# Attention and a state-space layer on one core: row maxima twelve steps ahead, other places for five groups of TensorE work, and the layer norm's Newton rounds moved from GpSimd to VectorE

## The reference, cut to what matters

```
# layer 0, per image, n = 4096 tokens, 32 query/key channels, 256 value channels
q, k, v = wq x + bq, wk x + bk, wv x + bv
attn    = softmax(q k, axis=-1)            # 4096 x 4096 per image
x1      = gamma * (v attn^T) + x
# layer 1, tokens of 256 channels
u  = (x1 - mean) * rsqrt(var + 1e-5) * norm_g + norm_b        # the layer norm
z, xBC, dt = split(in_w u);  xBC = silu(conv4(xBC) + conv_b)   # 4 groups of 128 channels
state = state * exp(dt*A) + (dt*x) B;  y = state C + Dp*x      # scan over the tokens
y = rmsnorm(y * silu(z)) * rms_w;  o = out_w y
out = x1 + o * sigmoid(se2(relu(se1(mean(o)))))
```

## Time and profile before

| what | value |
|---|---|
| median of three runs (lowest, highest) | 3107.33 us (3104.92, 3109.52) |
| time of the profiled execution | 3107.73 us |
| its span, first to last instruction | 3105.6 us |
| mean granted clock of TensorE | 0.979 of full speed |
| PE busy | 2928.8 us, 94% of the span |
| DVE busy | 2068.1 us, 67% |
| POOL busy | 1994.4 us, 64% |
| ACT busy | 1926.2 us, 62% |

### The profile page before, as it was taken

The page is one execution under the profiler, slowest core; times in us unless marked ns, Lnnn a source line. Parts: engine busy times, 40 slices in busy tenths (PEclk is TensorE's granted clock), DMA queues, the critical chain, the costliest instruction groups (busy, mean ns, idle before and its releaser), DMA issues. The chain is left out here.

```text
span 3105.6 us, 62448 instructions
## 1 busy us (share of the span) xinstructions
PE 2928.8 (94%) x20696; PEld 2256.1 (73%) x20696; DVE 2068.1 (67%) x3577; ACT 1926.2 (62%) x3806; POOL 1994.4 (64%) x3087
## 2 busy tenths in 40 slices
PE   6889999999999999999999999999999999999974
PEld 3767777777767777777777777777777777777752
DVE  5556666766766676666776667676766667776653
ACT  2556666666656666666665666666666666666642
POOL 2446665677665676666676666676777667777753
PEclk9999999999999999999999999999999999999985
DMA  3111111111311112122221122112121111112021
GB/s 121 53 32 43 47 58 58 32 49 55 98 71 65 58 65 89 68 78 75 91 84 37 65 72 87 65 68 89 40 90 36 50 64 45 68 50 70 35 96 68
DMA packets 102512, 200.94 MB, mean 65 GB/s; under 512 B 18768, under 2 KB 41936, under 8 KB 97808
## 3 DMA queue, kind: packets, MB, share of 16 engines
q1 hardware_dynamic: 98192, 195.08, 18.5%
q10 hardware_dynamic: 4000, 1.86, 0.2%
HBM read 131.21 MB, written 64.75 MB: 63 GB/s over the span
## 5 line engine op out<-in xcount | busy, mean ns | idle before, releaser
L727 POOL TENSOR_TENSOR p_lo<-p,p_hi 128x512 f16<-128x512 f32 x1024 | 1220.0, 1199 | 737.0 <-ACT p_hi L890 587.7
L883 ACT ACTIVATE p<-p_et 128x512 f32<-128x512 f32 x1024 | 614.6, 600 | 574.6 <-PE p_et L1141 511.1
L1159 PE MATMUL acc<-v_hi,p_hi 128*128 128x257 f16 x4096 | 954.5, 273 | 6.6 <-DVE work L1463 5.6
L1161 PE MATMUL acc<-v_lo,p_hi 128*128 128x256 f16 x4096 | 952.4, 273 | 0.0
L1419 DVE TENSOR_REDUCE maxes<-p_mx 128x1 f32<-128x1024 f32 x508 | 619.3, 1219 | 267.9 <-PE p_mx L1120 267.6
L890 ACT ACTIVATE p_hi<-p 128x512 f16<-128x512 f32 x1024 | 646.2, 631 | 8.3
L1167 PE MATMUL acc<-v_hi,p_lo 128*128 128x257 f16 x4096 | 622.8, 274 | 17.1 <-POOL p_lo L727 17.1
L1159 PEld LDWEIGHTS acc<-v_hi,p_hi 128*128 128x128 f16 x4096 | 403.6, 99 | 133.2 <-issue 71.8
L1161 PEld LDWEIGHTS acc<-v_lo,p_hi 128*128 128x128 f16 x4096 | 400.6, 98 | 103.3 <-issue 43.4
L1167 PEld LDWEIGHTS acc<-v_hi,p_lo 128*128 128x128 f16 x4096 | 399.9, 98 | 70.4 <-POOL p_lo L727 18.3
L1141 PE MATMUL p_et<-qs,kst 98*128 98x256 f16 x2048 | 393.1, 273 | 3.6 <-ACT p L883 2.9
(11 more groups left out here) (214 smaller groups left out, 4139.9 us busy)
## 6 DMA issues: line engine op xcount, KB each, us to landing
work<-rows_d SPq DMA_DIRECT2D x32, 1024.0 KB, 4.9
xin<-in_x_dram SPq DMA_DIRECT2D x48, 512.0 KB, 5.0
xr<-in_x_dram SPq DMA_DIRECT2D x32, 512.0 KB, 3.7
x_d<-x1c SPq DMA_DIRECT2D x31, 512.0 KB, 3.1
og_d<-og SPq DMA_DIRECT2D x29, 512.0 KB, 2.7
mix_x<-x_d SPq DMA_DIRECT2D x25, 512.0 KB, 4.7
mix_o<-og_d SPq DMA_DIRECT2D x24, 512.0 KB, 5.6
out_dram<-mix_o SPq DMA_DIRECT2D x24, 512.0 KB, 3.0
```

The source lines that it names most:

```text
L727: e.tensor_tensor(p_lo[:, n % RING, :], p32[:, n % P32S, :], p_hi[:, n % RING, :], ALU.subtract).then_inc(lo_pool, 1)
L883: e.activation(p32[:, n % P32S, :], p_et[:, :], ACT.Exp).then_inc(exp_done, 1)
L1159: e.matmul(acc[:, t, 0:C + 1], p_hi[:, r, at:at + P], v_hi[:, 2 * k + kk, 0:C + 1], start=(k == 0 and kk == 0), stop=False)
L1161: e.matmul(acc[:, t, 0:C], p_hi[:, r, at:at + P], v_lo[:, 2 * k + kk, :], start=False, stop=False, skip_group_check=True)
```

## The change

Four constants move fills: the third convolution group goes from step 20 to step 21, the first residual transpose from step 13 to step 5, the residual's bias from step 4 to step 2, and `AHEAD` goes from 10 to 12. With it the last pair of a half falls in step 2, the parts in step 4, and the first pair of the next half but one in step 4. As `K_MR` and `K_QR` get a new offset, the rows are filled in steps 7 and 23 and copied in steps 8 and 24. In slot 0 one more pair is computed early. The order of the fills in steps 3 to 9 becomes: x1T, x1T; y0, st0; xT; cb1; mr; y1, st1; uT, uT. By the rule of the two banks the xT now waits until y0 has been read (or, where there is one, the qk), and cb1 waits until st0 has.

The three Newton rounds of the layer norm are taken from POOL (14 operations) and written on DVE in step 3 (10 operations, a drain ahead of each). The semaphore from the guess to POOL goes away.

```diff
-K_XBC = (11, 16, 20, 26)
+K_XBC = (11, 16, 21, 26)
-K_XT = (13, 19)
-K_XB = 4
+K_XT = (5, 19)
+K_XB = 2
-AHEAD = 10
+AHEAD = 12
-K_PARTS, K_MR, K_QR = STEPS - AHEAD, STEPS - AHEAD + 2, STEPS - AHEAD + 3
+K_PARTS, K_MR, K_QR = STEPS - AHEAD, STEPS - AHEAD + 3, STEPS - AHEAD + 4
@@ pairs_at
-    early = {8: 0, 10: 1, 12: 2, 13: 3, 14: 4}
+    early = {8: 0, 9: 1, 10: 2, 12: 3, 13: 4, 14: 5}
@@ gpsimd
-            def norm(g):
-                e.wait_ge(ln_guess, g + 1)
-                e.tensor_scalar(nw[:, 2, :], mv[:, :, 0], -1.0, None, ALU.mult)
-                newton(nw)
-                e.tensor_tensor(nw[:, 4, :], nw[:, 2, :], nw[:, 3, :], ALU.mult).then_inc(ln_ready, 1)
@@ gpsimd step
-                if 0 <= s - 1 < G and K == K_LN + 2:
-                    norm(s - 1)
@@ vector stage_a
-                    rsqrt_guess(nw, nwi, mv[:, :, 1], 1.0, 1e-5).then_inc(ln_guess, 1)
+                    rsqrt_guess(nw, nwi, mv[:, :, 1], 1.0, 1e-5)
+                if K == K_LN + 2:
+                    for _ in range(3):
+                        e.drain()
+                        v.tensor_tensor(nw[:, 1, :], nw[:, 3, :], nw[:, 3, :], ALU.mult)
+                        e.drain()
+                        v.scalar_tensor_tensor(nw[:, 1, :], nw[:, 1, :], -0.5, nw[:, 0, :], ALU.mult, ALU.mult)
+                        e.drain()
+                        v.scalar_tensor_tensor(nw[:, 3, :], nw[:, 1, :], 1.5, nw[:, 3, :], ALU.add, ALU.mult)
+                    e.drain()
+                    v.scalar_tensor_tensor(nw[:, 4, :], mv[:, :, 0], -1.0, nw[:, 3, :], ALU.mult, ALU.mult)\
+                        .then_inc(ln_ready, 1)
```

More of the change, by code:

```diff
@@ L394, in conv_attention_mamba_kernel @@
         filled = sem("filled")
-        ln_guess = sem("ln_guess")
         ln_ready = sem("ln_ready")
```

## The result

| | before | changed |
|---|---|---|
| median of five runs (lowest, highest) | 3107.33 us (3104.92, 3109.52) | 3198.24 us (3188.55, 3201.65) |
| ratio with its 95% interval | 1 | 1.0289 [1.0274, 1.0305] |
| span of the profiled execution | 3105.6 us | 3195.2 us |
| mean granted clock | 0.979 | 0.969 |

The forecast was 3128 us, in 3082 to 3148. The sign and the first cause were right, the size was not: the loss is 4.4 times the one forecast.

A forecast was written before the change was run, and what follows sets the result against it. PE, busy 94% of the span, was taken as the bound, so only its idle time could be won. Terms -26.1 - 1.9 - 12.7 + 4 - 4.5 + 64.8 - 3 = +20.6 us on 3107.7 gave 3128 us, range 3082 to 3148.

The forecast's parts named there:

- the first cause: PE's new wait in step 5, for DVE to read y0, eats up more than is won; chance 0.57.
- What bounds the kernel, and what goes: PE busy 94% of the span; five waits inside the slots, 47.0 us together, could be won.
- the second rival: The cover holds: the ten Newton operations hide in DVE's 2.79 us gap and the slack behind it; 3063.5 us, chance 0.10.
- the third: The gain isn't there: group 2's product late by 1.1 us in step 26 instead of 0.2; 3148 us, chance 0.10.
- The wait for the parts: The rows' fill waits for the parts of the maximum; to go in all slots, -26.1 us, bounds 0 to -26.1.
- the state's reader in step 13: First residual transpose (xT) leaves the crowded step 13 and its wait there ends, -4.5 us.
- the one behind the rows' copy in step 9: Layer norm transpose's 3.7 us wait: rows copied in step 8 stand before the mixing operations, half saved, -1.9 us.
- Newton on DVE: Collisions with POOL make the chain 6.2 us; PE waits in step 5, 2.4 us in 24 slots, 1.8 in four: +64.8.
- Third group at 21: Product's wait in step 20 goes, -12.7 us; group 2's product 0.2 us late in step 26 in 21 slots, +4.
- Rows in steps 7 and 23: Rows three steps after the parts instead of two, so their fill's wait goes in all slots: -26.1 us.
- The clock: Rival: the granted clock falls after the 2.4 us waits, some 4 us more per slot in 28 slots; 3240 us, chance 0.04.
- the tail: After the slots, the layer norm's 4.5 us on POOL become 2.5 on DVE; -3 us taken.

## Why the prediction was wrong, step by step

*What bounds the kernel, and what goes.* Right. (One slip: no gain and no loss from the Newton rounds gives 3063.5, which is the second rival's time and not the third's.) The wait for the parts (26 us), for the product (12.7) and for the state's reader in step 13 (3.5 of 4.5) went. Beside these the wait at a half's start fell by 2.9 us and the one behind the rows' copy in step 9 by 3.4 (1.9 forecast): about 49 us in all, against 45 in the sum.

*Newton on DVE.* The mechanism was right and rather exact: 5.9 us for the chain against 6.2, six of ten operations held (the third `p_lo` meets op 8 and not op 7), and 1.86 us of waiting against 2.4; the slots that I called spared (1, 9, 17) were. The term was +64.8 us, measured +41.0. About 10 us of the difference are 0.5 us too much in each of 20 slots. The rest is in slots where the pattern of slot 6 doesn't hold: in slots 4, 12 and 20 a fill of query and key stands on PE just ahead and the wait is 0.6 and not 2.4, in slots 2, 10, 18 and 26 there is none in step 5 where I had 1.8 (in six of these seven PE waits 0.5 to 0.8 us in step 4 instead, 3.6 us in all), and in slot 31 it is 1.2. I had carried one slot over to all 28; that its rows repeat to a hundredth was true of the slots of its own kind only. This error ran against the others: with the chain priced at 41 us the forecast would have been 3104, further off still.

*Third group at 21: the step that failed first.* I gave the region of steps 22 to 26 +4 us, from DVE's free durations. It was 26 us, at another instruction: not the product but the exponential. I had used the rule of collisions for the new operations and not for the guess of the second norm, which already stood there, and I hadn't followed ACT, which is in order too and can't take the next exponential while it waits for tanh. The bound of 24 us was nearly right, though for another reason; the value chosen wasn't.

*Rows in steps 7 and 23: a step that was left out.* I priced the removed wait and not the new neighbours in the turn of the two banks. In slots with a value projection in step 7 the y of step 8 stands two places behind the rows and waits for their copy, which DVE takes behind the reduce of that same step (1.78 us, 8 times); in step 23 a value fill stands two places behind the other value fill of step 22 (1.74 us, 6 times). Both could be read off the list of fills as places to look at; together they are 24.6 us in the changed kernel. The run of the rows alone shows the first in full (14.2 us) and 6.3 us of the second, and with the guess one step later the second is 1.1 us, so the guess has a share in it.

*The clock: the right rival with the wrong form.* I took 2.1 us without a fall against 4.76 us with one as a choice between none and all, and gave it 0.04. In fact part of the waits of 1.8 us had a short fall behind them, at 1.7 us each: 22 of them, 34 us. This and the two steps above are +34 + 24.6 + 22; less the 24 us by which the chain was over-priced and 4 us of gain, they are 53 of the 69 us between the forecast and the profiled execution. The rest is in small things: about 9 us of other waits of PE (the 3.6 us of step 4 among them), 3 us of PE work beyond what the clock explains, and the 3 us that I took for the tail.

The Trainium skill (SBUF — State Buffer, section SBUF: two separate sides) says that a DVE operation with two inputs in SBUF and a GpSimd operation exclude each other for the whole instruction. The trace agrees: six of the ten were held to the end of a POOL operation, while the readers of y0 with one input in PSUM were not (0.41 us at 635.54 and 635.88 in the run with two rounds, beside `xsd`). The held operations aren't only those with two inputs: the guess's, at 709.71 and 710.75, read one tensor in SBUF and took 0.97 and 1.04 us. The Trainium skill (TensorE: Matmul & The Clock Gate, section Why this matters for your kernels) advises against long idle gaps between runs of matmuls; the trace goes further, with falls to 0.50 behind 13 of 20 gaps of 1.86 us or more.

What stays open: why the clock falls behind 13 of 20 nearly equal waits and not behind the other seven (with the guess one step later it falls behind 8 of them); and why the residual alone gains 14.5 us. The 4.5 of step 13, 3.5 at a half's start and 5 from the clock (118.6 us at the lower level, before 128.3) make 13, but the last may be chance: the run with the Newton rounds alone has 115.1 us there and no gain in time.

## What to carry to other kernels

A move is priced by what it does to every engine's in-order queue and to every buffer that is used in turn: write out the new order of users, and for each the reader that it now waits for. Two edits that cost nothing alone can meet in one wait, here a late reader and a fill that had just been bound to it, so try them together and apart. Short operations on VectorE with their inputs in SBUF cost what GpSimd happens to be doing, here 0.16 or 1.1 us, and each GpSimd operation that a chain of them behind drains meets holds up one of them; and a new wait of PE of 1.86 us cost nearly twice its length where TensorE's clock fell behind it.

## What the runs showed of the hardware that was not expected

Behind waits of 1.86 us or more, in which PE did nothing, the granted clock fell to 0.50 for 3.4 us in 13 slots of 20. With 16 matmuls that do nothing useful put into each of these waits none of the 13 falls came, and the whole kernel was 19.6 us faster. Seven operations in the Newton chain were 72 us cheaper than ten: the price was in the last three, whose neighbours on GpSimd stood back to back.
